# Turning the last block's relative values on the chip instead of through device memory, in an attention and feed-forward layer

## The chip, the cores and the metric

The kernel runs on one core of one Trainium2 chip. The metric is the device time of one execution in microseconds (us). Lower is better. One extra execution is recorded by the profiler; its rows are the ones read here.

## The reference

For x of shape (16, 256, 128) and xn = layernorm(x), the result is x + attention(xn) + ffn(xn). The feed-forward part has weights rounded to -1, 0 and 1. The attention has 16 heads of 8 values and relative positions for keys and for values:

```python
idx = clip(r[None, :] - r[:, None], -M, M) + M      # M = 128
content  = einsum('bhqd,bhkd->bhqk', q, k)
relative = einsum('bhqd,qkd->bhqk', q, rel_k[idx])
w = softmax((content + relative) / sqrt(8))
out = einsum('bhqk,bhkd->bhqd', w, v) + einsum('bhqk,qkd->bhqd', w, rel_v[idx])
y = out.reshape(B, S, D) @ Wo.T + bo
```

The last term of `out`, the relative values, is what the change is about.

## The kernel before

A first part computes the layer norm, the projections and the feed-forward part, and puts x plus feed-forward plus biases into device memory (`y_dram`). The main part goes over 8 slices of 32 queries (`qb`), and in each over 16 batch elements (`k`, a unit). A unit is one pass through scores (TensorE), maximum (VectorE), exponentials (ScalarE), a split of each into a high and a low half-precision part (`probs`), and the product with the values (`pv`), which VectorE adds up into `attT` (128 channels by batch by query; `own_pair`, `sum_pair`). All loops are unrolled, and each engine's order is written out by hand; semaphores are the only tie between engines.

Eight units are a block. There are 16 blocks, m = 2 qb + bg, where bg is the half of the batch. `relative` multiplies, query by query, the probabilities of a block with the relative values, in eight parts; four parts are a half and fill one PSUM bank `ps_r`. The bank's 128 partitions are 4 groups of 32 rows: 8 rows of high numerators, 8 rows of denominators (softmax sums), 8 of low numerators, 8 unused. Its 512 columns are query, batch and head. But `attT` has head and value index on the partitions and query and batch on the columns, so 32 rows and 32 columns have to be turned. The kernel before does this for each block by a trip through memory: ScalarE copies the bank to `rT` (`move_relative`, line 1167), SyncE's queue stores it in `rel_dram` (line 933) and loads it turned, in pieces of 128 bytes, into `land` (`load_relative`, line 944, four transfers a block). VectorE takes the reciprocal of the denominators in four pieces (`denominators`, line 1276), and GpSimd adds the high part, adds the low part and multiplies (`add_high`, `add_low`, `normalize`, lines 878, 883, 889).

For the last two blocks (14 and 15) VectorE does these three steps itself, half by half (`finish_half`, lines 1319, 1321 and 1324). The last block's load is issued in eight transfers of 64 KB from two queues (`load_last`, line 846), and it waits for the last store and for `att_ready` of block 13.

The output projection comes in four parts (`project(m)`, line 1108, 8 float32 products of 128 by 128, which the trace shows as 16 instructions), for (bg, half of the queries) = (0, 0), (1, 0), (0, 1), (1, 1). Part 2 needs block 14, part 3 block 15. `add_rest(m)` (line 1333) adds what `load_rest(m)` brought from `y_dram` (line 979), in two halves of 128 by 512, and `save_out(m, half)` (line 986) stores 256 KB of the output for each. VectorE's order at the end is

```python
add_rest(0); finish_half(14, 0); finish_half(14, 1); add_rest(1)
finish_half(15, 0); add_rest(2); finish_half(15, 1); add_rest(3)
```

and SyncE's is the stores of block 15, its loads, then the eight stores of the output.

## Time and profile before

| | |
|---|---|
| median of 3 runs | 462.95 us (462.84 to 466.07) |
| the profiled execution | 463.45 us |
| its span in the trace | 461.6 us |
| busy: TensorE, VectorE, ScalarE, GpSimd | 87%, 87%, 89%, 68% |

Times in the rows are from the start of the span. The profiled execution's own time is 1.85 us above its span, and 0.5 us above the median. Busy shares are means over the whole span; the change touches only what lies after 435 us.

### The profile page before, as it was taken

To read this page: it belongs to the slowest core of one execution; us is meant where nothing else is said; L and a number is where in the kernel's file an instruction comes from. 1 tells how busy PE (TensorE), PEld (TensorE's weight loads), DVE (VectorE), ACT (ScalarE), POOL (GpSimd) and SP (SyncE) were. 2 spreads that over 40 slices of the span, in tenths; PEclk is the share of its full clock that TensorE was granted. 3 is DMA by queue.
4 is the path that set the end of the run, shared out by engine and by line. 5 is a ranking of instruction groups with operands and counts; after the bars stand their busy time and mean duration, and the time that the engine had idled before them with its cause. 6 is when DMAs were issued, how large, how long until landed. Compare 5 with 4: busy or idle time off the path is not lost.

```text
span 461.6 us, 24715 instructions
## 1 busy us (share of the span) xinstructions
PE 403.2 (87%) x10258; PEld 333.2 (72%) x10258; DVE 400.1 (87%) x759; ACT 410.3 (89%) x806; POOL 314.1 (68%) x370
## 2 busy tenths in 40 slices
PE   0788888689999999989999999999999999999843
PEld 0345554478888888878888888888888887887643
DVE  8889766558988899989999999999999999998764
ACT  2889999559999999999999999999999999999700
POOL 6557787617675767877877778778777777776610
PEclk9999999889999999999999999999999999999996
DMA  7724744883112424434452424244352525246895
GB/s 162 238 47 122 126 93 126 159 148 86 25 40 54 79 55 86 77 75 72 73 96 49 86 47 85 61 74 90 71 78 66 92 44 89 55 81 94 164 208 157
DMA packets 159527, 43.08 MB, mean 93 GB/s; under 512 B 122320, under 2 KB 156600, under 8 KB 159288
## 3 DMA queue, kind: packets, MB, share of 16 engines
q1 hardware_dynamic: 152304, 40.19, 42.7%
q10 hardware_dynamic: 7112, 1.31, 1.7%
q8 instruction: 82, 1.34, 1.3%
q14 instruction: 29, 0.24, 0.2%
HBM read 21.55 MB, written 16.79 MB: 83 GB/s over the span
## 4 chain that ended last, share of the span: by engine, by line
ACT 43%; issue 20%; PE 12%; DVE 4%; POOL 1%; ACTq 0%; POOLq 0%; DVEq 0%
ACT big L1202 22%; ACT s L1160 9%; ACT ps_y L1182 7%; ACT p L1182 3%; PE ps_s L1025 2%; ACT xr L1167 2%; PE ps_s L1130 2%; PE ps_s L1030 2%; PE ps_o L1048 2%; PE ps_t L1118 1%; PE ps_r L1072 1%; DVE mcol L1286 1%; POOL big L871 1%; PE ps_s L1108 1%; DVE mx L1241 1%
## 5 line engine op out<-in xcount | busy, mean ns | idle before, releaser
L871 POOL TENSOR_TENSOR big<-p,big 128x512 f16<-128x512 f32 x128 | 148.2, 1158 | 91.8 <-ACT big L1202 91.1
L1025 PE MATMUL ps_s<-qbd,kst 96*128 96x128 f16 x1024 | 100.6, 221 | 8.8 <-ACT ps_y L1182 6.1
L1030 PE MATMUL ps_s<-by_q_room,e 96*128 96x64 f16 x2048 | 103.8, 193 | 0.0
L1286 DVE TENSOR_REDUCE mcol<-ps_t 128x4 bf16<-128x512 bf16 x128 | 87.9, 687 | 15.5 <-PE ps_t L1118 13.2
L1245 DVE TENSOR_TENSOR big<-ps_y,big 128x512 f16<-128x512 f32 x128 | 87.7, 685 | 6.9 <-ACT big L1202 6.1
L1241 DVE TENSOR_TENSOR mx<-s,ps_s 128x512 bf16<-128x512 bf16 x128 | 86.7, 677 | 3.6 <-ACT s L1160 2.5
L1160 ACT ACTIVATE s<-ps_s 128x512 bf16<-128x512 f32 x128 | 80.2, 627 | 8.3 <-PE ps_s L1030 8.0
L1030 PEld LDWEIGHTS ps_s<-by_q_room,e 96*128 96x128 f16 x2048 | 86.0, 98 | 0.0
L1202 ACT ACTIVATE big<-p 128x512 f16<-128x512 f32 x128 | 85.1, 665 | 0.0
L276 POOL COPY by_q_room<-qrel 96x256 uint32<-96x256 uint32 x128 | 79.1, 634 | 6.5 <-POOLq L300 3.1
L1182 ACT ACTIVATE ps_y<-ps_s 128x512 f32<-128x512 f32 x128 | 78.4, 612 | 4.5 <-PE ps_s L1130 3.4
L1130 PE MATMUL ps_s<-negid,mcol 128*128 128x128 bf16 x1024 | 79.1, 220 | 3.3 <-DVE mcol L1286 1.1
L1202 ACT ACTIVATE big<-ps_y 128x512 f16<-128x512 f32 x128 | 79.5, 621 | 0.0
L1182 ACT ACTIVATE p<-ps_s 128x512 f32<-128x512 f32 x128 | 78.9, 616 | 0.0
L1025 PEld LDWEIGHTS ps_s<-qbd,kst 96*128 96x128 f16 x1024 | 62.7, 98 | 14.4 <-ACT ps_y L1182 10.3
L1048 PE MATMUL ps_o<-big,v_sb 128*32 128x128 f16 x3072 | 66.6, 221 | 1.3 <-POOL big L871 1.0
L1130 PEld LDWEIGHTS ps_s<-negid,mcol 128*128 128x128 bf16 x1024 | 57.9, 98 | 7.7 <-DVE mcol L1286 7.0
L1118 PE MATMUL ps_t<-identb,mx 128*128 128x128 bf16 x512 | 51.3, 222 | 5.2 <-DVE mx L1241 2.8
L1048 PEld LDWEIGHTS ps_o<-big,v_sb 128*32 128x32 f16 x3072 | 44.1, 96 | 14.3 <-issue 1.3
L1072 PE MATMUL ps_r<-big,gv 128*24 128x128 f16 (+1 forms) x2048 | 50.0, 217 | 2.8 <-issue 1.6
L1118 PEld LDWEIGHTS ps_t<-identb,mx 128*128 128x128 bf16 x512 | 29.1, 98 | 23.3 <-DVE mx L1241 15.3
L1276 DVE RECIPROCAL xr<-xr 128x64 f32<-128x64 f32 x64 | 33.9, 539 | 3.8 <-DMA xr<-rel_dram 3.8
(110 smaller groups left out, 508.0 us busy)
## 6 DMA issues: line engine op xcount, KB each, us to landing
rel_dram<-xr SPq DMA_DIRECT2D x32, 256.0 KB, 2.5
xr<-rel_dram SPq DMA_DIRECT2D x60, 128.0 KB, 3.8
kst<-big SPq DMA_DIRECT2D x48, 64.0 KB, 2.0
qrel<-qr_dram SPq DMA_DIRECT2D x192, 16.0 KB
qbd<-q_dram SPq DMA_DIRECT2D x192, 16.0 KB
y_dram<-big SPq DMA_DIRECT2D x4, 512.0 KB, 2.9
big<-y_dram SPq DMA_DIRECT2D x4, 512.0 KB, 6.2
out<-big SPq DMA_DIRECT2D x8, 256.0 KB, 3.2
```

The costliest lines, as they stand in the source:

```text
L871: nc.gpsimd.tensor_tensor(probs[:, k // 8, 1, 1, k % 8, :], p32[:, k % 2, 1, :], probs[:, k // 8, 0, 1, k % 8, :], ALU.subtract).then_inc( ...
L1025: nc.tensor.matmul(bank[:, P * g:P * g + P], kst[:, g, S * k + P * kh:S * k + P * kh + P], rhs, start=(g == 0), stop=False, skip_group_che ...
L1030: ins = nc.tensor.matmul(bank.rearrange("p (h q j) -> p h q j", q=Q0, j=J)[:, :, q, :], e4[:, first:first + P], rhs.rearrange("p (h j) -> ...
L1048: ins = nc.tensor.matmul(ps_o[32 * g:32 * g + 32, room], val, probs[:, k // 8, x, kh, k % 8, P * g:P * g + P], start=(kh == 0 and x == 0 a ...
L1118: ins = nc.tensor.transpose(ps_tb[:, g, :], mx[:, P * g:P * g + P], identb[:, :])
L1130: ins = nc.tensor.matmul(ps_s[:, k % 2, kh, P * g:P * g + P], mcol[:, k % 2, g:g + 1].to_broadcast([P, P]), negid[:, :], start=False, stop ...
L1160: nc.scalar.activation(s0[:, :], ps_s[:, k % 2, 0, :], ACT.Copy).then_inc(half_copied, 1)
L1182: return nc.scalar.activation(dst.rearrange("p (g q h) -> p g q h", g=G, h=HH), ps_s[:, k % 2, kh, :].rearrange("p (g h q) -> p g q h", g= ...
L1202: nc.scalar.activation(probs[:, k // 8, 0, kh, k % 8, :], (ps_y[:, :], p32[:, k % 2, 1, :])[kh], ACT.Copy).then_inc((hi0_ready, hi_ready)[ ...
L1241: nc.vector.tensor_tensor(mx[:, :], s0[:, :], ps_s[:, k % 2, 1, :], ALU.max).then_inc(max_ready, 1)
L1245: nc.vector.tensor_tensor(probs[:, k // 8, 1, 0, k % 8, :], ps_y[:, :], probs[:, k // 8, 0, 0, k % 8, :], ALU.subtract).then_inc(lo0_ready, 1)
L1286: nc.vector.tensor_reduce(mcol[:, k % 2, :], ps_tb, X_AXIS, ALU.max).then_inc(mcol_ready, 1)
```

## The change

Block 15 no longer goes through memory. The second half of its relative values is written to bank `ps_y` rather than to `ps_r`, so that it needn't wait until `ps_r` has been copied. VectorE reads each bank of 128 by 512 with one 32 by 32 transposition (`turn`) into `rT`, takes the reciprocal of the 128 by 16 denominators, and spreads it over 128 by 128. TensorE turns `rT` back to channels on partitions with products by the identity (`turn_back`): high and low numerators into the bank's first 128 columns, reciprocals into the next 128. VectorE then needs one addition and one multiplication for each half (`finish`). ScalarE's two copies, two stores and eight loads of block 15 are gone. Block 14 still goes through memory, but its three steps are GpSimd's now. The parts of the projection and of the output come in the order 0, 1, 3, 2, and VectorE does all of its `add_rest` behind the rest; part 2 is computed in the banks that part 0 has used, part 3 in `ps_t` and `ps_o`.

```diff
@@ -786,7 +786,10 @@
     NT = TOK // P
     y_sb = v["big"][:, 0:NT * D].rearrange("p (t n) -> p t n", n=D)
     y_v, y_src = (t.rearrange("p (b h) d -> p h b d", h=KH) for t in (y_sb, y_dram))
-    banks = ((ps_s[:, 0, 0, :], ps_s[:, 0, 1, :]), (ps_s[:, 1, 0, :], ps_s[:, 1, 1, :]), (ps_t[:, :], ps_o[:, :]), (ps_s[:, 0, 0, :], ps_s[:, 0, 1, :]))
+    banks = ((ps_s[:, 0, 0, :], ps_s[:, 0, 1, :]), (ps_s[:, 1, 0, :], ps_s[:, 1, 1, :]), (ps_s[:, 0, 0, :], ps_s[:, 0, 1, :]), (ps_t[:, :], ps_o[:, :]))
+    OUT_ORDER = (0, 1, 3, 2)
+    identf = v["identf"]
+    inv = s0[:, 0:4 * H].bitcast(F32)
     out_t = out.rearrange("b (h p) d -> h p b d", p=P)
     ALL = NQB * UNITS
 
@@ -807,8 +810,8 @@
         rel_out = [sem(f"rel_out{i}") for i in range(2)]
         land_in = [sem(f"land_in{i}") for i in range(2)]
         rrden_ready, att_hi_added, att_lo_added, att_ready = sem("rrden_ready"), sem("att_hi_added"), sem("att_lo_added"), sem("att_ready")
-        last_in = [sem(f"last_in{i}") for i in range(2)]
-        last_hi_added, last_lo_added, last_ready = sem("last_hi_added"), sem("last_lo_added"), sem("last_ready")
+        turned, inv_ready, spread_ready, back_ready = sem("turned"), sem("inv_ready"), sem("spread_ready"), sem("back_ready")
+        last_added, last_ready = sem("last_added"), sem("last_ready")
         exp_ready, pv_ready, own_ready, out_summed = sem("exp_ready"), sem("pv_ready"), sem("own_ready"), sem("out_summed")
         wo_in = sem("wo_in")
         y_in = [sem(f"y_in{m}") for m in range(len(OUT_PARTS))]
@@ -836,14 +839,6 @@
             for m in range(BG * NQB - 3):
                 if UNITS * qb + k - 8 * m == steps[m < BG * NQB - 4]:
                     return m
-
-        def load_last(eng, half, groups):
-
-            m = BG * NQB - 1
-            eng.wait_ge(rel_out[half], 16 * (m + 1))
-            for g in groups:
-                src = rel_dram[m, g, half].rearrange("j (y d) (h n) -> (d h) j y n", d=HD, h=HH)
-                eng.dma_start(land[32 * g:32 * g + 32, m % 2, 4 * half:4 * half + 4, :, :], src).then_inc(last_in[half], 16)
 
         def block_of_att(m):
 
@@ -915,9 +910,10 @@
                     half_pair(nc, v, x, half)
             loop(pool, body)
             low_part(NQB - 1, UNITS - 1)
-            add_high(BG * NQB - 3)
-            add_low(BG * NQB - 3)
-            normalize(BG * NQB - 3)
+            for m in (BG * NQB - 3, BG * NQB - 2):
+                add_high(m)
+                add_low(m)
+                normalize(m)
 
         @block.sync
         def _(sp):
@@ -982,7 +978,7 @@
 
                 bg, qh = OUT_PARTS[m]
                 b0 = 8 * bg + 4 * half
-                sp.wait_ge(y_sum_ready, 2 * m + half + 1)
+                sp.wait_ge(y_sum_ready, 2 * OUT_ORDER.index(m) + half + 1)
                 sp.dma_start(out_t[qh, :, b0:b0 + 4, :], y_v[:, qh, b0:b0 + 4, :]).then_inc(y_sum_out, 16)
 
             last = BG * NQB - 1
@@ -993,14 +989,9 @@
             load_rest(0)
             load_rest(1)
             load_relative(last - 1)
+            load_rest(3)
             load_rest(2)
-            load_rest(3)
-            for half in range(2):
-                save_relative(last, half)
-            sp.wait_ge(att_ready, last - 1)
-            for half in range(2):
-                load_last(sp, half, range(0, 2))
-            for m in range(len(OUT_PARTS)):
+            for m in OUT_ORDER:
                 for half in range(2):
                     save_out(m, half)
             sp.wait_ge(y_sum_out, 16 * 2 * len(OUT_PARTS))
@@ -1053,7 +1044,9 @@
             def relative(qb, bg, part):
 
                 first, last = sum(REL_PARTS[:part]), sum(REL_PARTS[:part + 1])
-                if first % QH == 0:
+                ends = (qb, bg, first) >= (NQB - 1, BG - 1, QH)
+                bank = ps_y if ends else ps_r
+                if first % QH == 0 and not ends:
 
                     wait(pe, rel_moved, 2 * (BG * qb + bg) + first // QH)
                 if first == 0 and qb == 0 and bg == 0:
@@ -1069,7 +1062,7 @@
                         for j in range(4):
                             q = first - 4 * s + 4 * j + s
                             part_of = probs[:, bg, x, kh, :, :].rearrange("p b (g q h) -> p (b g) q h", g=G, h=HH)[:, :, q, :]
-                            ins = nc.tensor.matmul(ps_r[32 * j:32 * j + rows, own], gv[:, P * kh + S - 1 - q - QN * qb, 0:rows], part_of,
+                            ins = nc.tensor.matmul(bank[32 * j:32 * j + rows, own], gv[:, P * kh + S - 1 - q - QN * qb, 0:rows], part_of,
                                                    start=(first % QH == 0 and kh == 0 and x == 0), stop=(kh == KH - 1 and x == 1),
                                                    skip_group_check=True)
                 if last % QH == 0:
@@ -1088,21 +1081,32 @@
                         if 0 <= part < len(REL_PARTS) and not (back and isinstance(qb, int) and qb == 0):
                             relative(qb - back, bg, part)
 
+            def turn_back(half):
+
+                bank = (ps_r, ps_y)[half]
+                pe.wait_ge(turned, half + 1)
+                for low in range(2):
+                    nc.tensor.matmul(bank[:, 0:P], rT[:, half, 2 * P * low:2 * P * low + P], identf[:, :],
+                                     start=(low == 0), stop=False, skip_group_check=True)
+                pe.wait_ge(spread_ready, half + 1)
+                nc.tensor.matmul(bank[:, P:2 * P], rT[:, half, P:2 * P], identf[:, :], start=False, stop=True,
+                                 skip_group_check=True).then_inc(back_ready, 1)
+
             def project(m):
 
                 bg, qh = OUT_PARTS[m]
                 if m == 0:
                     pe.wait_ge(wo_in, 16 * H)
                     pe.wait_ge(exp_ready, ALL - 1)
-                pe.wait_ge(att_ready, (BG * NQB // KH, BG * NQB - 2)[qh])
+                pe.wait_ge(att_ready, (BG * NQB // KH, BG * NQB - 1 - bg)[qh])
                 if m == 1:
                     pe.wait_ge(exp_ready, ALL)
-                if m == 2:
+                if m == 3:
                     pe.wait_ge(mcol_ready, ALL)
                     pe.wait_ge(own_ready, ALL // 2)
-                wait(pe, last_ready, (0, 2 + 2 * bg)[qh])
+                    pe.wait_ge(last_ready, 2)
                 for half in range(2):
-                    wait(pe, y_sum_ready, 2 * (m - 3) + half + 1 if m == 3 else 0)
+                    wait(pe, y_sum_ready, half + 1 if m == 2 else 0)
                     for b in range(4):
                         b0 = 8 * bg + 4 * half + b
                         ins = nc.tensor.matmul(banks[m][half][:, P * b:P * b + P], attT[:, b0, P * qh:P * qh + P], wo_sb,
@@ -1145,9 +1149,10 @@
             pv(NQB - 1, UNITS - 1)
             for part in range(4, 8):
                 relative(NQB - 1, 1, part)
-            project(1)
-            project(2)
-            project(3)
+            for half in range(2):
+                turn_back(half)
+            for m in OUT_ORDER[1:]:
+                project(m)
 
         @block.scalar
         def _(act):
@@ -1225,11 +1230,6 @@
             exponentials(NQB - 1, UNITS - 1)
             high_part(NQB - 1, UNITS - 1, 0)
             high_part(NQB - 1, UNITS - 1, 1)
-            move_relative(NQB - 1, 1, 0)
-            move_relative(NQB - 1, 1, 1)
-            act.wait_ge(att_ready, BG * NQB - 2)
-            for half in range(2):
-                load_last(act, half, range(2, 4))
 
         @block.vector
         def _(dve):
@@ -1266,9 +1266,7 @@
 
             def denominators(m, piece):
 
-                if m == BG * NQB - 1:
-                    dve.wait_ge(last_in[piece // 2], 16 * G)
-                elif piece == 0:
+                if piece == 0:
                     dve.wait_ge(land_in[m % 2], 16 * LOADS * (m // 2 + 1))
                 if piece == 0:
                     wait(dve, att_ready, m - 1)
@@ -1308,27 +1306,36 @@
             maximum(0, 0)
             loop(dve, body)
 
-            def finish_half(m, half):
-
-                done = 2 * (m - (BG * NQB - BG)) + half + 1
-                x = slice(4 * half, 4 * half + 4)
-                sums = block_of_att(m)[:, x]
-                for piece in range(2):
-                    denominators(m, 2 * half + piece)
-                dve.wait_ge(out_summed, 4 * (m + 1))
-                nc.vector.tensor_tensor(sums, sums, landed(m, 0)[:, x], ALU.add).then_inc(last_hi_added, 1)
-                dve.wait_ge(last_hi_added, done)
-                nc.vector.tensor_tensor(sums, sums, landed(m, 2)[:, x], ALU.add).then_inc(last_lo_added, 1)
-                dve.wait_ge(last_lo_added, done)
-                dve.wait_ge(rrden_ready, 4 * m + 2 * half + 2)
-                nc.vector.tensor_tensor(sums, sums, reciprocals(m)[:, x], ALU.mult).then_inc(last_ready, 1)
+            def turn(half):
+
+                dve.wait_ge(rel_ready, 2 * (BG * NQB - 1) + half + 1)
+                dve.wait_ge(rel_out[half], 16 * (BG * NQB - 1))
+                nc.vector.transpose(rT[:, half, :].rearrange("p (y g d h) -> p g h y d", y=4, g=G, d=HD),
+                                    (ps_r, ps_y)[half][:, :].rearrange("p (n h) -> p h n", h=H)).then_inc(turned, 1)
+                dve.wait_ge(turned, half + 1)
+                den = rT[:, half, P:2 * P].rearrange("p (g d h) -> p g d h", g=G, d=HD)
+                own = inv[:, H * half:H * half + H].rearrange("p (g o h) -> p g o h", g=G, o=1)
+                nc.vector.reciprocal(own[:, :, 0, :], den[:, :, 0, :]).then_inc(inv_ready, 1)
+                dve.wait_ge(inv_ready, half + 1)
+                nc.vector.tensor_copy(den, own.to_broadcast([P, G, HD, HH])).then_inc(spread_ready, 1)
+
+            def finish(half):
+
+                bank = (ps_r, ps_y)[half]
+                sums = block_of_att(BG * NQB - 1)[:, 4 * half:4 * half + 4]
+                added, spread = (bank[:, P * i:P * i + P].rearrange("p (x s b) -> p x b s", x=4, s=4) for i in range(2))
+                dve.wait_ge(back_ready, half + 1)
+                dve.wait_ge(out_summed, ALL // 2)
+                nc.vector.tensor_tensor(sums, sums, added, ALU.add).then_inc(last_added, 1)
+                dve.wait_ge(last_added, half + 1)
+                nc.vector.tensor_tensor(sums, sums, spread, ALU.mult).then_inc(last_ready, 1)
 
             def add_rest(m):
 
                 bg, qh = OUT_PARTS[m]
                 dve.wait_ge(y_in[m], 16)
                 for half in range(2):
-                    dve.wait_ge(out_ready, 2 * m + half + 1)
+                    dve.wait_ge(out_ready, 2 * OUT_ORDER.index(m) + half + 1)
                     b0 = 8 * bg + 4 * half
                     nc.vector.tensor_tensor(y_v[:, qh, b0:b0 + 4, :], banks[m][half].rearrange("p (b n) -> p b n", b=4),
                                             y_v[:, qh, b0:b0 + 4, :], ALU.add).then_inc(y_sum_ready, 1)
@@ -1336,16 +1343,18 @@
             low_part(NQB - 1, UNITS - 1)
             for piece in range(4):
                 denominators(BG * NQB - 3, piece)
+            turn(0)
             own_pair(NQB - 1, UNITS - 1)
             sum_pair(NQB - 1, UNITS - 1)
-            add_rest(0)
-            for half in range(2):
-                finish_half(BG * NQB - 2, half)
-            add_rest(1)
-            finish_half(BG * NQB - 1, 0)
-            add_rest(2)
-            finish_half(BG * NQB - 1, 1)
-            add_rest(3)
+            turn(1)
+            finish(0)
+            for piece in range(2):
+                denominators(BG * NQB - 2, piece)
+            finish(1)
+            for piece in range(2, 4):
+                denominators(BG * NQB - 2, piece)
+            for m in OUT_ORDER:
+                add_rest(m)
 
 
 # ---- launch: one core; weights laid out with their input width first ----
```

## Rows read from the trace of the kernel before

**Rows 1.** The chain that ended last, its final pieces: start, length, what
```profile
446.61 7.96 issue
454.57 3.64 PE ps_s L1108 x16
458.21 0.02 issue
458.23 0.69 DVE big L1333
```

**Rows 2.** The waits between 434 and 462 us: total, times, longest
```profile
DVE xr L1276 <- DMA xr<-rel_dram: 3.8, 1, 3.8
```

**Rows 3.** Timeline, TensorE and ScalarE: start, busy, engine, line, tiles, count, idle before
```profile
433.89 2.05 PE L1108 MATMUL ps_s<-xr,attT 128*128 128x128 f32 x16
...
437.12 1.08 PE L1072 MATMUL ps_r<-big,gv 128*24 128x128 f16 x64 [0.73 <-POOL big L871]
...
438.01 0.52 PE L1048 MATMUL ps_o<-big,v_sb 128*32 128x128 f16 x24
438.24 0.60 ACT L1167 ACTIVATE xr<-ps_r 128x512 f32<-128x512 f32 x1 [2.50 <-PE ps_r L1072]
...
438.89 1.08 PE L1072 MATMUL ps_r<-big,gv 128*24 128x128 f16 x64 [0.36 <-ACT xr L1167]
```

**Rows 4.** Timeline, VectorE behind the last unit
```profile
435.86 1.78 DVE L1276 RECIPROCAL xr<-xr 128x64 f32<-128x64 f32 x4
...
439.04 0.42 DVE L1263 TENSOR_REDUCE attT<-own 128x64 f32<-128x256 f32 x1
439.37 1.28 DVE L1333 TENSOR_TENSOR big<-ps_s,big 128x512 f32<-128x512 f32 x2
440.57 0.96 DVE L1276 RECIPROCAL xr<-xr 128x64 f32<-128x64 f32 x2
441.44 0.27 DVE L1319 TENSOR_TENSOR attT<-attT,xr 128x128 f32<-128x128 f32 x1
441.75 0.37 DVE L1321 TENSOR_TENSOR attT<-attT,xr 128x128 f32<-128x128 f32 x1
442.15 0.38 DVE L1324 TENSOR_TENSOR attT<-attT,xr 128x128 f32<-128x128 f32 x1
...
449.42 0.96 DVE L1276 RECIPROCAL xr<-xr 128x64 f32<-128x64 f32 x2 [3.77 <-DMA xr<-rel_dram]
```

**Rows 5.** Timeline, GpSimd on block 13
```profile
436.93 0.96 POOL L878 TENSOR_TENSOR attT<-attT,xr 128x256 f32<-128x256 f32 x1
...
438.91 0.91 POOL L889 TENSOR_TENSOR attT<-attT,xr 128x256 f32<-128x256 f32 x1
```

**Rows 6.** Timeline of SyncE's queue: the time is that of issuing
```profile
435.62 0.89 SPq L944 DMA_DIRECT2D xr<-rel_dram  x1
...
444.97 2.07 SPq L846 DMA_DIRECT2D xr<-rel_dram  x4
447.08 12.24 SPq L986 DMA_DIRECT2D out<-big  x8
...
448.78 1.03 SPq L986 DMA_DIRECT2D out<-big  x1
...
458.95 0.37 SPq L986 DMA_DIRECT2D out<-big  x1
```

**Rows 7.** DMA in 436.5:437.3, 449.4:451 and 458:462: issue to landing, bytes
```profile
xr<-rel_dram SPq DMA_DIRECT2D x1, 128.0 KB, 4.4
...
DMA packets 1097, 0.53 MB, mean 334 GB/s; under 512 B 62, under 2 KB 1097, under 8 KB 1097
...
out<-big SPq DMA_DIRECT2D x1, 256.0 KB, 2.3
```

**Rows 8.** Windows: stretch, length, busy by engine, granted clock, DMA share, GB/s
```profile
440.00:443.00 3.00, 0.75 (x6) 0.66 (x7) 2.93 (x9) 0.60 (x1) 0.00 (x0) 1.00 1.16 320
...
451.00:454.50 3.50, 0.00 (x0) 0.00 (x0) 3.39 (x8) 0.00 (x0) 0.00 (x0) 0.51 0.86 253
454.50:458.30 3.80, 3.62 (x16) 3.46 (x16) 0.76 (x2) 0.00 (x0) 0.00 (x0) 0.55 0.09 25
```

## The prediction

> **What bounds the kernel now.** I read the chain that ended last first, because the shares of busy time (87 to 89% on three engines) are those of the main loop, and the change leaves the loop as it is. The chain ends with a gap of 7.96 us in which no engine works on it, a projection of 3.64 us, and one addition [rows 1]. The waits say what the gap is: VectorE stood 3.8 us for the loads of block 15 [rows 2]. The timelines give its story. The last values of block 15 are in PSUM when TensorE's second run of 64 products ends, at 438.89 + 1.08 = 439.97 [rows 3]. The turned loads are only issued at 444.97 [rows 6], and VectorE can start on them at 449.42 [rows 4]. So the trip costs 449.42 - 439.97 = 9.45 us. Behind it come two halves of arithmetic, a projection at a granted clock of 0.51 to 0.55 [rows 8], and the last store, issued at 458.95 and landed 2.3 us later, at 461.25; the span ends at 461.6 [rows 6, 7]. The windows show that TensorE had no instruction in 451 to 454.5, at a clock of about half (1.2 of 2.4 GHz) [rows 8].
>
> **Up to 438.2: nothing changes.** The loop, the first projection, the reciprocals of block 13 (435.86, four pieces) and the first half of block 15 have the same order on each engine. I cost this at nothing; it could carry some tenths of noise. The first half is ready when ScalarE's copy started, 438.24 [rows 3, 4].
>
> **TensorE.** The products with the values run 438.01 to 438.53, and the second 64 relative products then wait no more for ScalarE's copy (0.36 us idle before 438.89 [rows 3]): 438.55 to 439.6. The first projection's 16 instructions took 2.05 us, or 0.26 for each of 8 products [rows 3]; turning a half back is three such products, 0.77 us, and a projection stays 2.05.
>
> **VectorE's new steps.** No row has a transposition. Its nearest row by size is the addition of 128 by 512 from PSUM, 0.64 busy, or 0.60 from start to start (439.37 to 440.57 for two) [rows 4]; I take 0.68, the mean of single such additions (1.28 for two that overlap a little). Below that it can hardly be, as the same elements pass; above, I take double, 1.4, as the bound that counts for the range, since the read and the write are strided in float32. What the trace shows of strides argues for the low end: ScalarE's copy out of the same bank, reordered, took 0.60 [rows 3]. A step that needs the one before it starts some 0.03 us after that one's end (441.44 + 0.27 to 441.75 [rows 4]). The reciprocal of 16 columns lies between 0.11 (a quarter of the 0.44 us per piece of 64 [rows 4]) and 0.44; I take 0.2, nearer to the quarter, for the four pieces are long beside an addition twice as wide. Spreading 128 by 128 is like the 0.27 of an addition of that size, say 0.30 with its wait. Sum of a turn: 0.72 + 0.2 + 0.3 = 1.2 us. A `finish` is one addition and one multiplication of 128 by 128, 0.38 + 0.03 + 0.30 = 0.7 us [rows 4]; its operand in PSUM is strided, as above.
>
> The Trainium skill ("VectorE: DVE Perf Modes", The three transpose paths) gives 311 ns for 128 by 128 in bf16 on VectorE, and says that only blocks of 32 by 32 are turned. As an estimate from that page, four times this is 1.24 us, 0.56 more for each turn than my 0.68, and the sum would end 1.1 us later. No row here decides it.
>
> **VectorE's sequence** (one step behind the other, all waits met unless said). Turn(0) 438.24 to 439.44. The own-head product and sum of the last pair, 0.46 + 0.33: to 440.25; its products ended at 438.53, so it is now 0.9 us later than in the trace, and nobody needs it before `finish`. Turn(1), whose bank is full at 439.6: to 441.45. Finish(0): its products back are done by about 440.4: to 442.15. Two reciprocal pieces of block 14, 0.87 (440.57 to 441.44 [rows 4]): to 443.0. Finish(1): turned back by 442.0 to 442.2, so not waited for: to 443.75. The other two pieces: to 444.6. Then eight additions of the rest at 0.60: 444.6 to 449.5. Removed on VectorE against before are the four reciprocal pieces of block 15 and eight of the twelve steps of `finish_half` that were left; the gain, however, is the trip that VectorE stood waiting for, and the end.
>
> **Who could hold these additions up.** TensorE: turn_back(1) ends at 442.1, projection 1 at 444.1, projection 3 then has its last wait (finish(1), 443.8) behind it and ends at 446.15. Projection 2 needs block 14 on GpSimd. Its loads were issued last at 435.62 and landed 4.4 us later, at 440.0 [rows 6, 7]; GpSimd is free from block 13 at 439.8; its steps took 436.93 to 439.82 for three, with about 1.0 us each [rows 5]; the multiplication waits for VectorE's last piece, 444.6, and ends at 445.55. Behind this wait nothing is queued on GpSimd. So projection 2 runs 446.15 to 448.2, and the addition that wants its second half comes at 448.9. Slack 0.7 us. That the steps of block 14 pass from VectorE to GpSimd hides them; without that cover (GpSimd 1 us later) it is still the stores that end last, as follows.
>
> **SyncE and the stores.** Two stores and eight loads of block 15 leave the queues, about 1 MB in all, and the wait for block 13 with them. The swap of two loads of the rest moves nothing that is late: both were issued by 438.3. The first output store, which stood behind block 15's loads until 447.08 [rows 6], now goes at the end of the first addition, about 445.3. But now eight stores of 256 KB come at one every 0.60 us, which is 437 GB/s, and the rate that four back-to-back stores reach is 334 GB/s [rows 7]. So the stores, not VectorE, set the end: data flow from about 0.8 us after the issue (the share of the last store's 2.3 us that isn't 262144 B at 334 GB/s = 0.78 us, split before and behind). 445.3, plus 8 x 0.785 = 6.28, plus 2.3 - 0.78 = 1.5 us for latency, is 453.1 for the last landing, and 0.35 us on (461.25 to 461.6, above), 453.4, for the end. By VectorE alone it would be 449.5 + 2.3 + 0.35 = 452.2. That is the lower bound of this step.
>
> **The sum.** 461.6 - 453.4 = 8.2 us off the span. For the profiled execution that is 463.45 - 8.2 = 455.25; the median of the runs lies 0.5 us below it, so 454.7.
>
> The Trainium skill ("DMA: Bandwidth & Descriptors", Where 436 GB/s comes from) gives some 358 GB/s as the limit between a core and its device memory. By it the eight stores would take 5.9 us and the end come 0.4 us earlier; the row's 334 agrees with the kind of limit.
>
> **Rivals.**
> 1. *The transposition or the small steps cost more.* With 1.4 for each transposition and 0.45 for the reciprocal of 16, each turn costs 0.97 more. Everything on VectorE behind turn(0) moves, the first store too: +1.9 us, 456.6. For: strides, and no row. Against: the reordered reads seen at no price. Chance 0.20.
> 2. *TensorE's clock falls.* It stood at 0.51 after TensorE had been without work since 446.6, and it was 1.00 in 440 to 443 with 0.75 us busy of 3 [rows 8]. In the new order TensorE is idle only in pieces of under 1 us before 444. If it fell nevertheless, a projection costs 3.64 instead of 2.05 [rows 1, 3]: projection 3 from 445.7 (projection 1 later by 1.6) to 449.4, projection 2 to 453.0; the last addition 453.7, the end 2.65 behind it, 456.4, +3.0 us: 457.7. Chance 0.08. The skill's "TensorE: Matmul & The Clock Gate" (Part 1) has idle time bring the engine to 1.2 GHz, which is the rule that speaks against work in small pieces.
> 3. *Issuing the stores binds.* The fourth of the back-to-back stores took 1.03 us to issue [rows 6]. If all eight take that: 445.3 + 8.2 + 2.3 - 0.4 and 0.35 = 455.8, +2.4 us: 457.1. Against: it waited then behind small pieces of block 15's loads, which are gone. Chance 0.15.
> 4. *The stores don't queue.* The end by VectorE alone, 452.2, and steps a little shorter than taken, 0.5 us: 453.1. Chance 0.14.
> 5. *Slower.* The transposition isn't one pass over 512 columns but goes block by block, 16 blocks of 32 by 32, each at the price of a small instruction of its own. At the 0.27 us of the shortest VectorE row it is 4.3 us, and the two add 7.3: 462.0, no gain. At the 0.48 us of a reciprocal piece it is 7.7 and the two add 14.0: 468.7, slower by 1.2%. It decides from about 4.8 us per transposition, where 2 x 4.1 us eat the gain. Nothing in the profile speaks for it; only the lack of a row. Chance 0.03 for each of these two.
> 6. *It does less than it says*: the trip of block 14 stays, and the end waits for it as it waited for block 15. With the loads 4 us later than the 440.0 of the rows, VectorE's pieces of block 14 wait from 442.15 to 444.0, and all behind them is 1.85 us later: 456.6. Below 2 us of delay it costs nothing. The queue is the same up to there. Chance 0.03.
>
> **Chances and range.** Forecast 0.34 (454 to 455.5); the rest as above. A measurement of this kernel can tell about 1% (4.6 us) from no change. Faster by more than that means under 458.3: the forecast, 1, 2, 3, 4 and 6 all give it, less a part of 1, 2 and 3 in which two of them come together (0.05): 0.89. Within 1%: 0.08. Slower: 0.03. The range goes from 453.0 (case 4) to 457.8 (case 2, and case 1 with some of 3); outside are case 5 and the compounds.
>
> **What would show it.** Right: VectorE never idle for a DMA behind 438 us; a transposition group of two at 0.65 to 0.75 us; no ScalarE copy of `ps_r` and no line 846 behind 438; the first store issued at about 445.3; DMA at 330 GB/s or more from 446 to 452; the granted clock 1.00 until 448; the chain ending in a store, with its last addition near 449.5. Wrong: a transposition above 1 us (case 1), waits of VectorE for TensorE at the additions with a clock of half (case 2), issue times near 1 us on SyncE with the DMA below 300 GB/s (case 3), GpSimd's multiplication of block 14 behind 446.

## The result and the profile after

The change makes the kernel faster by 1.2%: 458.88 us, median of 4 runs (457.48 to 459.12), against 463.47 for the kernel before in the same comparison; the ratio is 0.988, 95% interval 0.984 to 0.993. In the second comparison, of 6 runs beside 11, it is 459.4, ratio 0.990 (0.987 to 0.993). Forecast were 454.7 and a range of 453.0 to 457.8. The sign was right, the size was forecast at 8.2 us and is about 4.6.

The profiled execution took 458.74 us, its span is 456.9. First the timeline of VectorE behind the last unit, which answers to [rows 4]:

```profile
437.16 1.78 DVE L1274 RECIPROCAL xr<-xr 128x64 f32<-128x64 f32 x4
...
439.54 1.18 DVE L1313 STREAM_TRANSPOSE xr<-ps_r 128x512 f32<-128x512 f32 x1 [0.60 <-PE ps_r L1065]
...
440.75 0.25 DVE L1318 RECIPROCAL s<-xr 128x16 f32<-128x16 f32 x1
...
441.04 0.23 DVE L1320 COPY xr<-s 128x128 f32<-128x128 f32 x1
441.18 0.42 DVE L1253 TENSOR_TENSOR own<-ps_o,hmask 128x256 f32<-128x256 f32 x1
...
441.97 1.07 DVE L1313 STREAM_TRANSPOSE xr<-ps_y 128x512 f32<-128x512 f32 x1
...
443.50 0.28 DVE L1329 TENSOR_TENSOR attT<-attT,ps_r 128x128 f32<-128x128 f32 x1
...
444.02 0.96 DVE L1274 RECIPROCAL xr<-xr 128x64 f32<-128x64 f32 x2
...
446.23 2.42 DVE L1340 TENSOR_TENSOR big<-ps_s,big 128x512 f32<-128x512 f32 x4
...
449.76 1.28 DVE L1340 TENSOR_TENSOR big<-ps_s,big 128x512 f32<-128x512 f32 x2
```

The 3.8 us wait for a DMA is gone [rows 2], and so is the gap of 7.96 us [rows 1]. VectorE goes through to 451.04. But two things catch the eye. The reciprocals of block 13 start at 437.16, not 435.86, although nothing ahead of them was changed. And between the last addition, 451.04, and the end of the span lie 5.86 us, where the kernel before had 2.68. That stretch is the stores. From the issue of the first one, 446.89, to the end of the span it is 10.0 us, where 8.1 were forecast. The queue's timeline, and the windows (stretch, length, busy by engine, granted clock, DMA share, GB/s), which answer to [rows 6] and [rows 8]:

```profile
446.89 0.38 SPq L982 DMA_DIRECT2D out<-big  x1
...
447.49 0.38 SPq L982 DMA_DIRECT2D out<-big  x1
...
448.08 1.92 SPq L982 DMA_DIRECT2D out<-big  x1
```

```profile
447.50:449.50 2.00, 1.99 (x18) 1.79 (x17) 2.00 (x4) 0.00 (x0) 0.00 (x0) 1.00 0.87 237
449.50:450.50 1.00, 0.00 (x0) 0.00 (x0) 1.00 (x3) 0.00 (x0) 0.00 (x0) 1.00 0.20 48
...
452.00:453.00 1.00, 0.00 (x0) 0.00 (x0) 0.00 (x0) 0.00 (x0) 0.00 (x0) 1.00 1.02 290
453.00:454.00 1.00, 0.00 (x0) 0.00 (x0) 0.00 (x0) 0.00 (x0) 0.00 (x0) 1.00 1.03 291
```

The third store took 1.92 us to issue, so that the DMA engines had next to nothing in 449.5 to 450.5 (48 GB/s), and behind it the stores ran at about 290 GB/s to the end, not at the 334 of [rows 7].

TensorE (the timeline, answering to [rows 3]) stopped between the two passes of one float32 product, although what it reads, the copy of 441.04, had long been done:

```profile
440.77 0.71 PE L1089 MATMUL ps_r<-identf,xr 128*128 128x128 f32 x4
...
441.32 0.38 PE L1092 MATMUL ps_r<-identf,xr 128*128 128x128 f32 x1
...
442.91 0.38 PE L1092 MATMUL ps_r<-identf,xr 128*128 128x128 f32 x1 [1.22 <-issue]
```

"issue" says that nothing the profile shows was waited for. In this execution VectorE came to its first `finish` at 443.50, just behind it, and lost nothing.

### The profile page after: what moved, and what is told of

Read it like the earlier page. It is cut to its first block, busy times and chain, and to the rows that moved or that the text cites. A ratio compares the mean times of both kernels' runs of the same rounds, so it can differ in the third digit from the quotient of the medians.

```text
span 456.9 us, 24721 instructions
## 1 busy us (share of the span) xinstructions
PE 403.1 (88%) x10270; PEld 333.2 (73%) x10270; DVE 398.6 (87%) x753; ACT 409.0 (89%) x804; POOL 316.9 (69%) x373
## 3 DMA queue, kind: packets, MB, share of 16 engines
q8 instruction: 82, 1.34, 1.3%
## 4 chain that ended last, share of the span: by engine, by line
ACT 43%; issue 17%; PE 13%; DVE 5%; POOL 1%; ACTq 0%; DVEq 0%; POOLq 0%
ACT big L1207 21%; ACT ps_y L1187 9%; ACT s L1165 9%; PE ps_s L1016 3%; PE ps_s L1134 2%; ACT p L1187 2%; PE ps_s L1021 2%; ACT xr L1172 2%; PE ps_o L1039 2%; PE ps_t L1122 2%; PE ps_r L1065 1%; DVE mcol L1284 1%; DVE mx L1241 1%; DVE big L1340 1%; PE ps_r L252 1%
## 5 line engine op out<-in xcount | busy, mean ns | idle before, releaser
L1065 PE MATMUL ps_r<-big,gv 128*24 128x128 f16 x1984 | 49.1, 217 | 3.7 <-issue 3.0
L1065 PEld LDWEIGHTS ps_r<-big,gv 128*24 128x24 f16 x1984 | 32.7, 90 | 5.0 <-issue 4.9
```

## The experiments

Since the loop's length differs between executions, traces are compared from the start of the last four reciprocals of block 13 (T0). "Stop" is TensorE's idle time at the place just shown. The kernels were timed in groups, each beside the kernel before, so that across groups the ratios count and not the medians. Times in us.

| kernel | T0 | stop | last addition ends, from T0 | span ends, from T0 | median | ratio to before (95%) |
|---|---|---|---|---|---|---|
| before | 435.86 | | 23.06 | 25.74 | 463.47 | |
| before_again | 437.33 | | 22.21 | 24.97 | 464.06 (one) | |
| pool_14 | 436.44 | | 22.69 | 25.46 | 463.64 | 1.000 (0.998 to 1.002) |
| the change | 437.16 | 1.22 | 13.88 | 19.74 | 458.88 | 0.988 (0.984 to 0.993) |
| after_again | 437.33 | 2.59 | 15.88 | 21.07 | 459.4 | 0.990 (0.987 to 0.993) |
| after_third | 437.40 | 1.35 | 14.54 | 20.50 | 459.71 (one) | |
| two_queues | 437.48 | 2.32 | 15.51 | 20.02 | 457.61 | 0.987 (0.984 to 0.990) |
| quarter_stores | 438.51 | 2.16 | 16.17 | 18.09 | 456.18 | 0.983 (0.979 to 0.986) |
| thin_rest | 435.59 | 0.26 | 14.53 | 20.01 | 457.61 | 0.986 (0.983 to 0.989) |
| plain_turn | 437.05 | 2.17 | 15.11 | 19.75 | 458.75 | 0.988 (0.984 to 0.992) |
| early_rest | 435.34 | 1.10 | 15.48 | 18.36 | 457.36 | 0.985 (0.982 to 0.988) |
| early_first | 437.52 | 0.27 | 13.80 | 17.88 | 456.67 | 0.984 (0.981 to 0.987) |
| early_mid | 437.47 | 0.82 | 15.38 | 18.23 | 457.23 | 0.987 (0.985 to 0.989) |

**before_again: the loop.** No edit.

> A second trace of the kernel before. Theory (the main loop's length differs from one execution to the next, and the profiled one of the kernel before was short): the first projection starts at 434.3 to 436.5, not at 433.89, and the tail from the reciprocals of block 13 to the end is 25.7 us within 0.4. Rival (the changed kernel's loop is longer by 1.3 us for a reason of its own): 433.9 within 0.3.

T0 is 437.33, 1.47 later than in the first trace of the same code, and the first projection starts at 435.37. The loop's length is a matter of the execution: T0 lies between 435.34 and 438.51 in thirteen traces, with changed and unchanged tails alike. The tail fell by 0.8 us against the first trace, more than the 0.4 I allowed.

**after_again, after_third: the same code.** No edit.

> The changed kernel once more, for a second trace and as the base of this group. Theory (the end is set by the output stores, at 290 GB/s and with a hole of 0.9 us while the third store is issued): 457 to 459 us, first addition of the rest to last landing 9.5 to 10 us again, with the hole again. Rival (the hole and the low rate are an accident of one execution): no hole, 334 GB/s, some 1.5 to 2 us less in that stretch. Second question: how much later the loop ends than the 433.9 us of the kernel before. If that is accident, the first projection starts anywhere in 433.5 to 435.5.

> A third trace of the changed kernel: how often TensorE's stop (1.2 and 2.6 us so far) and the slow issue of the third store (1.9 and 2.0 us) come. Theory (the stop goes with the loads): a stop of 1 to 2.7 us again; tail from the reciprocals of block 13 to the end 19.5 to 21.2 us. For the slow issue I have no theory beyond that it belongs to the place in SyncE's stream: then 1.5 us or more for the third store again.

The slow third store came all three times (1.92, 2.04 and 2.02 us to issue), and so did 290 GB/s; so the first rival falls. The stop came with 1.22, 2.59 and 1.35 us. At 2.59 it costs twice: VectorE waits, and the granted clock is down behind it. The timeline first, then the window:

```profile
444.46 0.38 PE L1092 MATMUL ps_r<-identf,xr 128*128 128x128 f32 x1 [2.59 <-issue]
...
444.87 0.29 DVE L1329 TENSOR_TENSOR attT<-attT,ps_r 128x128 f32<-128x128 f32 x1 [1.10 <-PE ps_r L1092]
...
445.34 3.38 PE L1112 MATMUL ps_s<-xr,attT 128*128 128x128 f32 x16
```

```profile
445.50:449.00 3.50, 3.50 (x20) 3.50 (x19) 3.47 (x9) 0.00 (x0) 0.85 (x1) 0.51 0.01 2
```

The first shows VectorE 1.10 us idle at its first `finish` and a projection of 3.38 us instead of 1.95; the second the granted clock, 0.51 in 445.5 to 449, so 1.2 GHz, behind that stop.

At 1.35, in after_third, the stop cost nothing: VectorE did not wait at its first `finish`. Yet its last addition ended 0.66 us later from T0 than in the first trace (14.54 against 13.88). The timeline has the reason one step earlier, in the spreading of the first half's reciprocals:

```profile
441.27 0.84 POOL L873 TENSOR_TENSOR attT<-attT,xr 128x256 f32<-128x256 f32 x1
441.28 0.91 DVE L1320 COPY xr<-s 128x128 f32<-128x128 f32 x1
```

This copy takes 0.23 us elsewhere. It took 0.91 to 0.93 us in three traces (after_third, quarter_stores, thin_rest), where GpSimd's addition for block 14 had begun 0.01 us before it, and 0.76 and 0.56 us in early_rest and plain_turn, where an instruction of GpSimd was under way; in all five it ended 0.08 us behind GpSimd's. In the other five new tails, and for the second half in all ten, GpSimd had at most 0.05 us left to run when it began, and it took 0.23. That VectorE's copy was held by GpSimd's instruction is read from these coincidences; no run moved GpSimd's addition. It is up to 0.7 us of VectorE's path that the prediction has no term for.

**quarter_stores: are the stores the end?** Each store takes 64 of its 256 KB; three quarters of the output are left out.

```diff
-                sp.dma_start(out_t[qh, :, b0:b0 + 4, :], y_v[:, qh, b0:b0 + 4, :])...
+                sp.dma_start(out_t[qh, :, b0:b0 + 1, :], y_v[:, qh, b0:b0 + 1, :])...
```

> Each store takes only 64 of its 256 KB; three quarters of the output are left out. Theory (the stores' bytes set the end): the end goes back to the last addition, some 451.0, plus the latency of one store of 64 KB, 1.7 to 2.0, and 0.35: span about 453.3, 3.5 us less than the changed kernel. Rival (VectorE and TensorE set the end, the stores are hidden but for the last): under 1 us less.

From the last addition to the end it is 1.92 us in place of 5.86, 5.19 and 5.96, and the median is 3.2 us below that of the change in the same group (456.18 against 459.4). The 2 MB of stores are what ends last (their pieces fell to a quarter together with their bytes, so the two aren't told apart). What comes up behind them is TensorE: the chain of this kernel's end is its projections, the first of them (shown from about 448 on) at the lower clock.

```profile
447.83 2.54 PE ps_s L1112 x13
450.37 0.89 PE ps_t L1112 x8
451.26 0.89 PE ps_o L1112 x8
452.15 1.80 PE ps_s L1112 x16
```

**two_queues: the slow issue.** The second half of each part is stored from ScalarE's queue.

```diff
             def save_out(m, half):
+                if half == 1:
+                    return
...
+            for i, m in enumerate(OUT_ORDER):
+                bg, qh = OUT_PARTS[m]
+                b0 = 8 * bg + 4
+                act.wait_ge(y_sum_ready, 2 * i + 2)
+                act.dma_start(out_t[qh, :, b0:b0 + 4, :], y_v[:, qh, b0:b0 + 4, :]).then_inc(y_sum_out, 16)
```

> The second half of each part is stored from ScalarE's queue, the first from SyncE's. Theory A (issuing on one queue makes the hole: the third store took 1.92 us to issue): the hole goes, and the last landing comes 0.9 to 1.5 us earlier, about 457.5 us. Theory B (the DMA engines' rate of 290 GB/s alone): no change within 0.4 us, since the bytes are the same.

All eight stores were issued in 0.37 to 0.39 us each, the hole was gone, and from last addition to end it took 4.51 us, with a stop of 2.32 us in the same trace. The median fell by 1.8 us in the same group (457.61 against 459.4; the intervals of the two ratios overlap by a little). The rate stayed at 273 to 295 GB/s. So theory A holds for the hole and B for the rate. What makes the third issue slow is not shown: in plain_turn, on one queue, it took 0.51 us, in thin_rest 1.47.

**early_rest: start stores earlier.**

```diff
+            add_rest(0)
             turn(0)
...
-            for m in OUT_ORDER:
+            for m in OUT_ORDER[1:]:
                 add_rest(m)
```

> The additions of part 0, which are ready from 437.2 on, move from behind all else on VectorE to ahead of the first turn. VectorE does the same work but fills 0.6 us in which it waited for TensorE; two of the eight stores start 7 us earlier. Theory (stores bind): last addition 0.6 us earlier, six stores left to do behind it instead of eight: the end by bytes is the first late addition (446.8) + 0.8 + 6 x 0.9 + 0.7 = 453.8, by VectorE 450.4 + 2.3 = 452.7: the span falls by 2.5 to 3.5 us, to about 456 us in time. Rival (VectorE alone binds): 0.6 us less. Rival (turn(0) later delays the chain): 0 or 0.6 us more.

The median is 2.0 us below the change in the same group, the tail 18.36 against 19.74 to 21.07, with six stores behind the first late addition. This trace has a stop of 1.10 us and the fallen clock too (0.50 from 442.5 to 445.5), and VectorE waited for the projections at its last additions (15.48 from T0); the stores had become short enough to hide that no more.

**thin_rest: where the stop comes from.** The two loads for parts 2 and 3 bring an eighth of their rows, so the result lacks the rest.

```diff
                 bg, qh = OUT_PARTS[m]
-                sp.dma_start(y_v[:, qh, 8 * bg:8 * bg + 8, :], y_src[:, qh, 8 * bg:8 * bg + 8, :])...
+                n = 1 if m > 1 else 8
+                sp.dma_start(y_v[:, qh, 8 * bg:8 * bg + n, :], y_src[:, qh, 8 * bg:8 * bg + n, :])...
```

> The two loads for parts 2 and 3 of the output bring 64 KB each instead of 512, so seven eighths of their rows are missing in the result. In three of four traces of this family TensorE stood 2.2 to 2.6 us between the two passes of one product by the identity, at the fifth instruction behind the relative products, while these two loads filled the DMA engines, and its clock then fell to half. Theory (the instruction stream's own transfer is held up by these loads): the stop shrinks under 0.5 us, the clock stays at 1.00, VectorE no longer waits 0.7 to 1.1 us at its first finish, and the median is 1 to 2 us below that of the changed kernel (459.4). Rival (the stop has nothing to do with the loads): stop and clock as they were, time unchanged.

Of the five traces up to then it was three, not three of four, that had a stop of 2.2 to 2.6 us. Here the stop shrank to 0.26 us and the clock stayed (window below: 1.00, and a DMA share of 0.01). The time shows it less well. The median is 1.8 us below after_again's, in another group; the ratios, 0.986 (0.983 to 0.989) and 0.990 (0.987 to 0.993), overlap, so that a gain of the forecast 1 to 2 us isn't shown. In the trace the tail is 20.01 us and the last addition ends at 14.53, no better than the 19.74 and 13.88 of the change's first trace: here the copy took 0.91 us.

```profile
441.07 0.38 PE L1093 MATMUL ps_r<-identf,xr 128*128 128x128 f32 x1 [0.26 <-issue]
```

```profile
439.00:445.00 6.00, 4.45 (x42) 3.70 (x31) 5.76 (x16) 0.00 (x0) 2.13 (x3) 1.00 0.01 1
```

The length of a stop is also a matter of when TensorE comes to the place: at 4.5 us from T0 in the change's first trace, at 5.2 in thin_rest, where the late copy had kept it. So the point at which it goes on is the better measure. From T0 that is 5.48 us in thin_rest, 5.21 in early_first and 5.76 in early_mid (the two kernels with the loads issued earlier, below), and 6.45 to 7.40 in nine of the other ten traces. The tenth is the change's first, with 5.75.

The DMA page shows what was held up. In all traces one packet of 16 KB (82 of them carry 1.34 MB over the whole span) of the queue "instruction" passes ahead of the stop's end. Here it is in 0.2 us windows of the change (from 439.8) and of after_again (from 441.8):

```profile
q8 instruction: 1, 0.02, 47.3%
```

```profile
q8 instruction: 1, 0.02, 32.5%
```

TensorE goes on at 442.91 and 444.46, 3.0 and 2.6 us later. In thin_rest it is 438.3 and 441.07, in early_first 440.1 and 442.73, and over all thirteen traces 2.3 to 3.0 us lie between. What differs is when the packet passes: 2.6 to 3.2 us from T0 with the loads thin or earlier, 4.1 to 4.8 in the nine traces, 2.7 in the change's first. In that one the two loads were issued 1.35 us behind T0, in the nine 0.7 to 1.0; that the packet slipped in ahead of them there is my reading, not tested.

The place is always behind the fifth product after the relative ones in the new tails, and behind the fourth in the kernel before and pool_14, where it falls into the second projection, which nobody waits for (2.25, 2.53 and 1.71 us there). The Trainium skill ("Runtime: NRT & Kernel Launch", Instruction fetch mechanics) says that each engine's instructions come in blocks of 16 KiB by a DMA queue of its own, and that crossing a block is mostly hidden. The packet's size agrees; the profile doesn't name the engine that a packet is for. "Mostly hidden" doesn't hold at this place, least of all with the DMA engines full of loads.

**plain_turn: the transposition's price.**

```diff
-                nc.vector.transpose(rT[:, half, :].rearrange("p (y g d h) -> p g h y d", ...),
-                                    (ps_r, ps_y)[half][:, :].rearrange("p (n h) -> p h n", h=H))...
+                nc.vector.transpose(rT[:, half, :], (ps_r, ps_y)[half][:, :])...
```

> Both transpositions read and write their 512 columns in order, not reordered by head, so the relative values of block 15 end up in wrong places. Theory (strides make it 1.07 to 1.18 us): 0.60 to 0.70 each, the last addition 0.9 us earlier. Rival (the transposition of four-byte data out of PSUM costs this in any order): 1.05 to 1.2 us as before, no change of time.

```profile
439.42 0.72 DVE L1313 STREAM_TRANSPOSE xr<-ps_r 128x512 f32<-128x512 f32 x1 [0.60 <-PE ps_r L1065]
...
441.73 0.70 DVE L1313 STREAM_TRANSPOSE xr<-ps_y 128x512 f32<-128x512 f32 x1
...
444.24 0.29 DVE L1328 TENSOR_TENSOR attT<-attT,ps_r 128x128 f32<-128x128 f32 x1 [1.26 <-PE ps_r L1092]
```

In order it takes 0.72 and 0.70 us; the reordering costs 0.4 each. The time, however, hardly moved (458.75): what VectorE saved it lost at the stop, where it now waited 1.26 us. The last addition came at 15.11 us from T0, not 0.9 us earlier as I expected.

**pool_14: one part alone, in the kernel before.** The waits of the last projections are changed to match, which isn't shown.

```diff
-            add_high(BG * NQB - 3)
-            add_low(BG * NQB - 3)
-            normalize(BG * NQB - 3)
+            for m in (BG * NQB - 3, BG * NQB - 2):
+                add_high(m)
+                add_low(m)
+                normalize(m)
...
-            for half in range(2):
-                finish_half(BG * NQB - 2, half)
+            for piece in range(4):
+                denominators(BG * NQB - 2, piece)
```

> The kernel before, with only the three steps of block 14 moved to GpSimd. Theory (the end waited for the trip of block 15 and nothing else): the load of block 15 is issued on the same signal, so the end moves by less than 0.5 us; VectorE only waits longer for it. Rival (VectorE's load in the tail was a part of the price): 1 us or more less.

463.64 against 463.48: nothing, within 1 us by the interval (0.998 to 1.002). VectorE's wait for the loads grew from 3.8 to 4.4 us. So the gain comes from the trip, not from moving block 14's steps off VectorE.

**early_first: both remedies together.** From early_rest:

```diff
-            load_relative(last - 1)
             load_rest(3)
             load_rest(2)
+            load_relative(last - 1)
```

> As early_rest, and the loads for parts 2 and 3 are issued ahead of the load of block 14. If the loads hold up TensorE's instructions, the stop shrinks and the clock stays. The price: block 14 lands some 3 us later, at about 444 in place of 441, where VectorE wants it at 443. Sum by the theory: 1 to 2 us less than early_rest (457.36), about 455.8. Rival (block 14 is late and everything stands behind it): 457.4 to 458.5, VectorE waiting on a DMA at the reciprocals of block 14.

456.67 us, ratio 0.984 (0.981 to 0.987) to the kernel before: the shortest tail (17.88) and the lowest median of the kernels that compute everything. Beside the change's 0.988 to 0.990 the intervals still touch, and beside early_rest's 0.985 (0.982 to 0.988) they overlap almost wholly: the median is 0.7 us lower, where 1 to 2 were expected, so what the second remedy adds in time isn't shown. What it does in the trace is: the stop is 0.27, the clock 1.00. The price was a wait of 0.35 us:

```profile
445.18 0.96 DVE L1274 RECIPROCAL xr<-xr 128x64 f32<-128x64 f32 x2 [0.35 <-DMA xr<-rel_dram]
```

**early_mid: one step more.** From early_first:

```diff
-            for half in range(2):
-                turn_back(half)
-            for m in OUT_ORDER[1:]:
+            turn_back(0)
+            project(1)
+            turn_back(1)
+            for m in OUT_ORDER[2:]:
                 project(m)
...
             finish(1)
+            add_rest(1)
             for piece in range(2, 4):
                 denominators(BG * NQB - 2, piece)
-            for m in OUT_ORDER[1:]:
+            for m in OUT_ORDER[2:]:
                 add_rest(m)
```

> From early_first: TensorE computes part 1 of the projection ahead of turning the second half back, while it waits for that half's transposition, and VectorE adds part 1 right behind its second finish. Two more of the eight stores start 1.5 us earlier. Theory (what is left is bytes of stores and the chain of the last two projections): the last addition 0.5 us earlier or equal, four stores behind it instead of six, the end 0.5 to 0.8 us below that of early_first, 456.0 in time. Rival (moving the projection delays the second finish and so both last projections by up to 1 us): 456.7 to 457.5.

457.23: no gain, and my sum was wrong. The time lies in the rival's range, but not by its mechanism. The second finish came on time (8.6 us from T0, 8.5 in early_first). But the last two pieces of block 14 moved behind two additions, GpSimd's multiplication with them, and the last projection waited for it:

```profile
450.08 2.05 PE L1112 MATMUL ps_s<-xr,attT 128*128 128x128 f32 x16 [1.20 <-POOL attT L884]
```

The stop was 0.82 us, with the loads as early as in early_first.

## Why the prediction was wrong, step by step

The mechanism was right: the end waited for the trip of block 15 (pool_14), the trip went, and the eight stores became the end (quarter_stores). The size was little over half of the forecast. What failed is the last term, the 6.28 us for the stores at 334 GB/s; beside it the sum had no line for TensorE's stop and none for the held copy. For the profiled execution the difference can be settled to some tenths. Forecast was a span of 453.4; it is 456.9.

- *"Up to 438.2: nothing changes"* was costed "at nothing; it could carry some tenths of noise". It carried 1.3 us (T0 437.16 against 435.86). This is no effect of the change: before_again has 437.33. The one profiled execution on which all was built had a short loop. The same mistake stands in "the median of the runs lies 0.5 us below it": here the median is 0.14 above the profiled execution. Together 1.9 us of the 4.2 us between 454.7 and 458.88. It says little of why the gain is 4.6 and not 8.2, for in that the loop's spread is on both sides.
- *VectorE's sequence.* Forecast from T0 to the end of the first late addition: 9.4 us; measured 9.7. The transposition, taken at 0.68 with 1.4 as upper bound, took 1.18 and 1.07, so case 1 was right by half: ScalarE's reordered copy at no price, my ground for the low end, says nothing about VectorE's transposition (plain_turn: 0.72 in order). The estimate of 1.24 from the Trainium skill's figure ("VectorE: DVE Perf Modes", The three transpose paths) came nearer, but by luck: it scales with size alone, and at this size the transposition in order took 0.72. The reciprocal took 0.25 (0.2), the copy 0.23, but 0.91 in after_third. What I took too dear made up for it: a `finish` takes 0.5 us, not 0.7. Error of the step: 0.3, and 0.66 more where the copy was held.
- *"The stores, not VectorE, set the end"*: right, and this is the term of the sum that was mis-sized, by 1.9 us. The rate is 290 GB/s, which makes 7.23 us of the 6.28; the other 0.9 is the hole behind the third store. It is the same in all three traces of the change: 10.0, 10.1 and 10.1 us from the issue of the first store to the end, for the 8.1 forecast. The 334 GB/s of [rows 7] came from the one stretch of four stores in the kernel before. Its single stores at the end reached no more than about 290, and I didn't look:

  ```profile
  450.50:451.00 0.50, 0.00 (x0) 0.00 (x0) 0.44 (x2) 0.00 (x0) 0.00 (x0) 1.00 1.15 345
  ...
  458.60:459.00 0.40, 0.00 (x0) 0.00 (x0) 0.32 (x1) 0.00 (x0) 0.00 (x0) 1.00 1.00 292
  ```

  Case 3 named the slow issue, with another size and place.
- *"Who could hold these additions up: TensorE."* Projection 1 was put down at 442.1 to 444.1, without a row for the stop, though it was in view in the second projection of the kernel before. I took it for a wait whose reason didn't matter:

  ```profile
  442.86 1.50 PE L1108 MATMUL ps_s<-xr,attT 128*128 128x128 f32 x12 [2.25 <-issue]
  ```

  In this trace it cost nothing, in after_again 1.1 us of waiting and, with the clock of case 2, 1.4 us of projection.
- *Case 2, the clock.* I gave it 0.08, on the ground that TensorE would be idle only for pieces under 1 us. The clock stayed at 1.00 to 454 in the profiled execution and through the projections of after_third, and fell to half in after_again behind a stop of 2.59 us. A stop is idle time that this ground left out, so 0.08 was too low. The stop's length doesn't decide alone: the clock fell behind 2.59, 2.53, 2.32, 2.17 and 2.16 us, and in early_rest behind 1.10, but not behind 2.25 (the kernel before), 1.71, 1.35 or 1.22.
- *GpSimd for block 14*: multiplication at 446.46 to 447.32 (behind the 446 named as a sign of being wrong, but only by the 1.3 us of the loop), 0.2 us before the last projection began (447.54). That projection's end, 449.49, lay 0.9 us ahead of the addition that wanted it, for a forecast slack of 0.7. Block 15's traffic and block 14's landing (forecast 440.0 for the trace before) held nothing up; case 5 and case 6 did not come.

Sum of the span: 1.3 + 0.3 + 1.9 = 3.5 us, which is 456.9 - 453.4. Over executions, tails fell from 25.74 and 24.97 to 19.74, 21.07 and 20.50, some 4.9 us, against 8.2. That is the shortfall of the gain: 1.9 to 2.0 us of stores in each trace, 0.3 of VectorE's steps, and by trace nothing more, 1.2 of the stop or 0.66 of the held copy ahead of the first store; the rest is that the tail of the kernel before was 0.8 us shorter in its second trace.

Open stay why the third store's issue is slow in some kernels, why four stores of the kernel before ran at 340 GB/s (again in pool_14 and before_again) where the new tails ran at 273 to 295, and what else than its length decides whether a stop brings the clock down. None was tried further.

## What to carry to other kernels

When a wait of 8 us at the end goes, work that lay in its shadow comes to lie bare: here 2 MB of stores, and a stop of TensorE, by all signs for its instructions. Cost these by their own rates before the gap is booked as gain, and spread the stores. An idle time marked "issue" in the trace before, even one that costs nothing there, needs its own line in the sum if the change puts something urgent behind it. And one profiled execution is one draw: with a loop of 430 us that varies by 3 us, a forecast to 1% needs the spread of the tail and of the loop apart.

## What the runs showed of the hardware

- A 32 by 32 transposition of 128 by 512 float32 from PSUM on VectorE takes 0.70 to 0.72 us in order and 1.03 to 1.18 us when reordered by heads on both sides.
- At one place in its stream TensorE stopped for 1.1 to 2.6 us while 1 MB of loads was in flight; with the loads gone (0.26 us) or issued earlier (0.27 and 0.82) for less. It went on 2.3 to 3.0 us behind a packet of 16 KB of the queue "instruction", at 6.45 to 7.40 us from T0 in nine traces with the loads in flight (5.75 in a tenth) and at 5.21 to 5.76 in the three others. That the one waits for the other is argued from thirteen such pairs; no run moved the block's boundary.
- A copy of 128 by 128 float32 on VectorE took 0.23 us, and 0.56 to 0.93 us where an instruction of GpSimd was running, ending 0.08 us behind that one in all five cases. No run tested it.
- Stores of 256 KB in pieces of 512 bytes ran at 273 to 295 GB/s in the new tails, from one queue or two.
